# Experts' part without POOL's drain, VectorE's order in the last block, and queries turned ahead of the last value rows

## The reference

```python
x = x + _L0_xattn_ref(_layernorm(x), ctx, ...)        # 16 heads of 64
x = x + _L0_ffn_ref(_layernorm(x), ...)               # 8 experts, top 2, and a shared one
x = x + _L1_xattn_ref(_layernorm(x), ctx, ctx, ...)   # 16 heads of 16
x = x + _L1_ffn_ref(_layernorm(x), weight, bias)      # fp8 rounding with one scale for all of x
```

```python
Qp = query @ Wq + bq
K = _l2norm(key @ Wk + bk); V = value @ Wv + bv; Q = _l2norm(Qp)
attn = softmax(Q K^T / 4) over 16 heads
x = attn V @ Wo + bo + Qp
(x - mean) / sqrt(var + 1e-5) * ln_gamma + ln_beta
```

## Time and profile before

| | before |
|---|---|
| median of 3 runs | 942.38 us (939.27 to 947.75) |
| profiled execution, time | 947.8 us |
| its span | 946.0 us |
| TensorE busy | 867.4 us, 92% |
| VectorE busy | 723.1 us, 76% |
| ScalarE busy | 527.6 us, 56% |
| GpSimd busy | 366.6 us, 39% |

### The profile page before, as it was taken

One profiled execution on the slowest core, in us unless ns is written; L12 is line 12 of the kernel. 1 busy time (PEld: TensorE's weight loads), 2 busy tenths in 40 slices (PEclk: granted clock), 3 DMA queues, 4 the chain that ended last, 5 costly groups with the idle time before them and its releaser, 6 DMA issues. The chain is left out here.

```text
span 946.0 us, 18647 instructions
## 1 busy us (share of the span) xinstructions
PE 867.4 (92%) x5904; PEld 793.7 (84%) x5904; DVE 723.1 (76%) x1821; ACT 527.6 (56%) x1454; POOL 366.6 (39%) x412
## 2 busy tenths in 40 slices
PE   5899999999999999999979999996899999999435
PEld 5889999999999988898978999995688888888324
DVE  6788788878878978878656677784525889877888
ACT  4776567656747645546244444443435566664277
POOL 3234333424333426756521211413544757431230
PEclk9999999999999999999999999997768999999758
DMA  9999970000100013434125434434111111000003
GB/s 287 311 336 326 333 229 0 0 0 0 34 0 1 1 34 96 127 108 140 62 85 146 122 110 148 141 124 122 35 50 35 51 40 46 23 1 2 0 22 156
DMA packets 51771, 91.89 MB, mean 97 GB/s; under 512 B 5381, under 2 KB 26298, under 8 KB 51697
## 3 DMA queue, kind: packets, MB, share of 16 engines
q1 hardware_dynamic: 45105, 72.87, 24.0%
q0 software_dynamic: 6592, 18.07, 6.1%
HBM read 34.56 MB, written 56.36 MB: 96 GB/s over the span
## 5 line engine op out<-in xcount | busy, mean ns | idle before, releaser
L535 POOL TENSOR_TENSOR prob<-prob,row_inv 128x462 f32<-128x462 f32 (+1 forms) x96 | 83.8, 875 | 178.8 <-DVE row_inv L711 178.8
L898 PE MATMUL acc<-u,probT 128*128 128x256 f32 (+1 forms) x960 | 134.2, 289 | 1.0 <-DVE u L723 1.0
L595 ACT ACTIVATE prob<-score,neg_max 128x77 f32<-128x77 f32 x512 | 121.2, 353 | 13.3 <-DVE neg_max L705 12.9
L851 PE MATMUL score<-m,xnT 128*128 128x462 f32 (+1 forms) x576 | 122.7, 350 | 0.0
L898 PEld LDWEIGHTS acc<-u,probT 128*128 128x128 f32 (+1 forms) x960 | 119.5, 189 | 1.9 <-DVE u L723 1.4
L851 PEld LDWEIGHTS score<-m,xnT 128*128 128x128 f32 x576 | 96.3, 188 | 5.8
L2128 PEld LDWEIGHTS acc<-vz,prob 128*128 128x128 f32 (+1 forms) x640 | 82.4, 203 | 13.0 <-issue 11.2
L1231 PE MATMUL py<-w1T,hidT 128*128 x426 | 93.0, 354 | 0.0
L585 ACT ACTIVATE probT<-tr 128x512 fp32r<-128x512 f32 (+1 forms) x96 | 52.0, 545 | 66.2 <-PE tr L837 65.8
L1676 POOL DMA_INDIRECT dispatched<-xn,slots x64 | 69.5, 1085 | 43.8 <-DVEq L1460 26.5
L2128 PE MATMUL acc<-vz,prob 128*128 128x34 f32 (+2 forms) x640 | 84.4, 287 | 0.0
(11 more groups left out here) (381 smaller groups left out, 2100.5 us busy)
## 6 DMA issues: line engine op xcount, KB each, us to landing
dispatched<-zeros SPq DMA_DIRECT2D x1, 33664.0 KB, 109.2
xn<-dispatched SPq DMA_DIRECT2D x71, 128.0 KB, 2.0
dispatched<-hid SPq DMA_DIRECT2D x71, 128.0 KB, 1.8
out<-x_res SPq DMA_DIRECT2D x7, 512.0 KB, 2.6
x_res<-in_x SPq DMA_DIRECT2D x1, 3072.0 KB, 15.2
consts<-in_L_ffn_W SPq DMA_DIRECT2D x8, 384.0 KB, 3.5
consts<-in_L_ffn_Ws SPq DMA_DIRECT2D x3, 384.0 KB, 3.6
x_res<-in_x SPq DMA_DIRECT2D x2, 512.0 KB, 10.2
```

Of the source, the lines that this page charges most:

```text
L535: gp.tensor_tensor(pr, pr, row_inv[t % 2][:, heads(k)].unsqueeze(2).to_broadcast([P, BANK_HEADS[k], KEYS]), ALU.mult).then_inc(prob_ready, 1)
L595: last = act.activation(prob[t % 2][:, h * KEYS:(h + 1) * KEYS], score_of(t, k)[:, n * KEYS:(n + 1) * KEYS], ACT.Exp, bias=neg_max[t % 2][ ...
L851: last = pe.matmul(score_of(t, k)[:, 0:BANK_HEADS[k] * KEYS], xnT[blk][i][:, dc, j * P:(j + 1) * P], m[w][:, dc, cols(k)], start=(n == 0 a ...
L898: last = pe.matmul(acc[t % 2][:, 0:D], probT[t % 2][i][0:rows, c, :], u[k][0:rows, c, :], start=(c == 0 and q == 0), stop=(c == KCH - 1 an ...
```

## The change

Three things are changed. The Block of the experts' part is made without POOL's drain: its barrier then has no `Drain` of POOL, the other engines still drain and report, and POOL still releases them once it has come there itself. In the last block VectorE adds beta for the last two blocks behind the query residual, returns from `dve_block` behind gamma, and does the last units ahead of the shift and update; a maximum of an older block takes the place of a younger one, which moves towards the end. In the opening TensorE turns block 0's queries and does the first scores ahead of value rows 16 to 19, and VectorE splits the queries ahead of the products of these rows.

```diff
-        with nc.Block() as block:
+        with nc.Block(no_gpsimd_drain=True) as block:
...
             dve_query_residual(dve, n)
+            if not nxt:
+                dve_beta(dve, LAST - 1)
+                dve_beta(dve, LAST)
             if nxt:
                 dve_queries(dve, n + 1, 1)
...
             dve_gamma(dve, n - 1, 1)
+            if not nxt:
+                return
             if prv3:
                 dve_last_max(dve, n - 3)
             dve_beta(dve, n - 1)
-            if not nxt:
-                dve_beta(dve, LAST)
             dve_update(dve, n - 1)
...
                 dve_shift(dve, 1)
-                dve_value_rows(dve, range(16, len(SPREAD)))
                 for dc in range(DC):
                     dve_split_q(dve, 0, dc)
+                dve_value_rows(dve, range(16, len(SPREAD)))
                 dve_query_residual(dve, 0)
...
-                dve_last_shift(dve, LAST - 2)
                 for a in range(2):
                     dve_inverse(dve, LAST, 1, a)
                     dve_unit(dve, LAST, 1, a)
+                dve_last_shift(dve, LAST - 2)
+                dve_update(dve, LAST - 1)
                 dve_last_stats(dve, LAST - 1)
-                dve_last_max(dve, LAST - 2)
+                dve_last_max(dve, LAST - 3)
                 dve_residual(dve, LAST, 0)
...
                 dve_last_stats_half(dve, 1)
+                dve_last_max(dve, LAST - 2)
+                dve_last_shift_half(dve, 1)
                 dve_last_max(dve, LAST - 1)
                 dve_last_max_half(dve, 0)
-                dve_last_shift_half(dve, 1)
...
-                pe_value_rows(pe, range(4, len(SPREAD)))
+                pe_value_rows(pe, range(4, 16))
                 for dc in range(DC):
                     pe_transpose_q(pe, 0, dc)
                 pe_scores(pe, 0, 0)
+                pe_value_rows(pe, range(16, len(SPREAD)))
                 pe_first_block(pe)
```

## The result

| | before | changed |
|---|---|---|
| median (14 runs each) | 942.36 us (932.58 to 949.81) | 930.80 us (926.61 to 938.80) |
| profiled execution, time | 947.8 us | 929.04 us |
| its span | 946.0 us | 927.0 us |
| mean granted clock in it | 0.951 | 0.961 |

The account below looks back on a forecast made before the run. TensorE is full in most of the program, so time is won only where it stands still or runs at half speed. Terms -7.0 - 3.9 - 0 to 1.6 - 3.8 against the median 942.4 give 927 us; range 920 to 933.

Parts of the forecast that it names:

- Part 1: Experts' end: without POOL's drain the barrier opens at about 650.5 instead of 657.5, so TensorE starts 7.0 us earlier.
- Part 4: Last block: beta additions hidden in VectorE's idle time, last units wait only for TensorE's last values; -3.8 us.
- Part 2: Opening of the second attention: clock stays up through the shorter pause, so 8.3 us of low-clock work become 4.4; -3.9 us.
- Part 3: Opening: queries turned when ready, rows 16 to 19 behind the first scores; -1.6 to 0 us, nearest prices +0.5 and -2.
- Block 0: Second attention's first block: clock expected to fall again at the turns in most runs, so no gain counted there.
- rival A: Block 0: the clock doesn't fall at all, winning 10 us more, for 921.5 us; chance 0.22.
- B: Experts' end: POOL's 7 us come out again ahead of its next gather, costing 3.7 us, for 931 us; chance 0.12.
- D: Not faster: the clock falls at the turns and stays low until block 1 is over, 953 us; chance 0.02.
- C: Last block: its gain isn't seen, moved additions or ACT's order hold the last units; 3.8 us, 931 us; chance 0.05.

Follow-up runs that it names:

- drain_only: The kernel before with only the experts' Block ended without POOL's drain; 944.30 us, ratio 0.9924 [0.9878, 0.9970].
- no_open_again: The changed kernel with the opening's old order put back, on the second chip; 934.30 us, ratio 0.9848 to the kernel before.
- gathers_late: The kernel before, drain kept, with the experts' part's last six gathers issued in the second attention instead; 957.60 us, ratio 1.0040.
- no_open: The changed kernel with the opening's old order put back, on the first chip; 937.38 us, ratio 0.9881 to the kernel before.
- after_filled: The changed kernel with useless matmuls in TensorE's two waits around the turns of the opening's queries; 920.48 us, ratio 0.9744 to the kernel before.
- before_again: The kernel before itself, unchanged, run and profiled again on the third chip; 943.06 us, ratio 0.9995.
- filled_tail: after_filled with useless matmuls also in TensorE's waits of the last part; 935.86 us, ratio 0.9813 to the kernel before.
- no_open_filled: no_open_again with useless matmuls in the two waits around the first scores; 923.56 us, ratio 0.9771 to the kernel before.
- filled_drain: after_filled with POOL's drain put back at the experts' end; 945.39 us, ratio 0.9897 to the kernel before.
- filled_tail_bar: filled_tail with four 128x128 matmuls on TensorE ahead of the experts' barrier; 934.78 us, ratio 0.9794 to the kernel before.

## Why the prediction was right, and where it was wrong

Parts 1 and 4 came as forecast. What failed is the size of the sum, and in it two steps of the opening: Part 2 took the full clock behind the short pause for certain (-3.9), and Part 3 priced the turned order at -1.6 to 0 against an opening that the other edits had changed. In the profile that goes with the result the two together gave -2.5 us at the second scores, for a forecast of -3.9 to -5.5.

**Part 1, right.** The barrier opened 0.1 us behind SP's drain, and TensorE's pause went from 8.3 to 1.4 us: -6.9 for a forecast of -7.0. drain_only has -7.0 as a whole, with 2.9 to 11.6 allowed by its interval, so that this match is partly luck. POOL gave nothing of it back where anybody waits; its drain at the program's end took 8.50 us instead of 5.46.

What was said to cost nothing did so with less cover than thought. VectorE's first additions started 1.9 us behind the first turn, about as forecast (1.7 us behind the barrier), but took longer. Timeline of VectorE, changed kernel:

```profile
650.98 4.70 DVE L2342 SCALAR_TENSOR_TENSOR x_res<-routed,share,x_res 128x256 f32<-128x256 f32 x4 [2.86 <-DMA routed<-dispatched,slots]
...
656.59 0.68 DVE L2357 TENSOR_TENSOR qp<-proj,bq 128x512 f32<-128x512 f32 x1
...
659.65 1.66 DVE L2342 SCALAR_TENSOR_TENSOR x_res<-routed,share,x_res 128x256 f32<-128x256 f32 x4
```

Four additions took 4.70 us here, and the next four, from 659.65 on, 1.66 us. The excess sits in a single one. All eight of these, by line (ns min/median/max):

```profile
L2342 DVE SCALAR_TENSOR_TENSOR x_res<-routed,share,x_res x8: 475/480/3507, 651.0 to 660.8; 128x256 f32<-128x256 f32 x8
```

It lasted from 651.38 to 654.89. With the drain gone it lies beside POOL's two products at 651.88 and 653.21 (1.39 and 1.38 us). In the kernel before, the first additions lay beside a gather of POOL (658.22) and were over ahead of these products, and took 1.67 us: so the gathers' issue is not what holds them up. The other side of it is a gain: qres took 3.52 us beside the next two of these products, and now comes behind them (671.75) and takes 1.22. The bias on the first queries then starts at 656.59, 1.4 us behind their end (655.2), where I had VectorE free by then. The second half's bias follows at 659.05, 2 us behind its product, so part of the distance to the unit queries is probably VectorE's and not TensorE's. The Trainium skill (SBUF — State Buffer, Who interferes with whom) has the rule that a VectorE instruction with two SBUF inputs contends with a GpSimd instruction that reads SBUF, and the trace agrees: 4.70 us beside POOL's products, 1.66 without. The prediction applied it to the additions of beta, where POOL is idle, and to qres, and not to the one place where the change newly puts the two engines side by side.

**Part 2, the step that failed first.** "The clock was still at 1.00 for 2.9 us after work stopped, so it should now stay up." In 8 of the 12 profiled executions in which the drain was gone or hidden it did. In 4 (the first of the changed kernel, drain_only, no_open_again, gathers_late) it fell within 0.3 us of the first turn, for 3.4, 10.2, 3.4 and 3.4 us. In the first three the unit queries were then turned at +14.91, +19.50 and +16.31, against +13.59 and +14.99 where it stayed. So -3.9 was the best case and not a middle: a fall of 3.4 us cost 1.3 us, one of 10.2 us 4.5. The size where it holds is right: 17.31 - 13.60 = 3.7 in the pair that differs in nothing else ahead of the turns. The Trainium skill (TensorE: Matmul & The Clock Gate, Part 1: The HAM clock gate) says that the chip judges past activity and not program positions; the prediction quoted it, said that the 3.9 us "may be lost again in single runs", and took nothing off for it.

**Part 3, mis-sized, with the wrong base.** It was costed at -1.6 to 0 as a change to a slow opening. Once Parts 1 and 2 are made, the opening as it was is a different one: at full clock rows 16 to 19 take 1.99 us (no_open) and end 1.4 us behind the moment at which the turned order can turn. What is left to win is 1.4 us. In the low clock that comes earlier with it, 2.1 us or more are lost between first and second scores (5.1 to 5.3 us against 3.0 in no_open; it was 3.4 before). The term is +0.7 to +1.4 at the second scores, by three profiles of each order. The bound of the prediction, +0.5, was a little short of it. The second scores came 2.5, 4.0 and 3.3 us nearer to the first turn, for a forecast of 3.9 to 5.5.

**Block 0, right in kind.** The clock fell again about the turns in all three profiles of the changed kernel: with the first scores in two, in the wait ahead of the turns in the third, for 13.7 to 17.1 us, and later for 6.8. So rival A's condition never came about. Its price can't be read directly: after_filled still fell once, for 6.8 us, and from its second scores to block 2's queries it has 28.25 us against 36.89 and 34.12 in the two profiles of before, 8.6 and 5.9 less, for A's 10. The base was a poor one: that profile had 34.2 us at the low clock in block 0, the second 27.4. And A's 921.5 is worked from the profiled 947.8 while the forecast, B and D go by the median; from 942.4 it would have been 916.1, below the range that was to hold it.

**Part 4, right within 0.2 us.** From block 2's queries to x_amax the changed kernel needs 178.72 to 178.74 us in three profiles, and the kernel before 182.30 and 182.39: -3.6, made of -3.8 up to the last turn and +0.2 behind it. From the last values to x_amax it is 19.27 instead of 23.08 us in the first pair, -3.8. The maximum of block LAST-2 stands at 878.58 without a wait ahead of it, as forecast.

**The other rivals.** B is out by POOL's rows above, C by the last turn's 0.81 us, and D by every profile of the changed kernel, whose block 1 was never low to its end: in the first the clock was at 1.00 from 696.95 to 864.23.

**The sum.** From the first turn to the end the changed kernel has 277.93, 276.67 and 277.16 us, before_again 285.71: -7.8 to -9.0, with the pause -14.7 to -15.9, which is the forecast sum. That it comes out is in part luck. Up to the second scores it is -2.5 to -4.0 instead of -3.9 to -5.5, and from there to block 2's queries another -1.8 to -1.9 (32.2 to 32.3 against 34.1), for which the sum had nothing: the shorter falls in block 0 paid for what Parts 2 and 3 lacked. The last part, x_amax to the end, is 0.3 to 0.4 us longer.

The medians have -11.6, -13.6 and -13.8, so 2 to 4 us less than the profiles. The profiled executions of the changed kernel are 0.8 to 2.8 us under their medians, and those of the kernel before 1.2 to 5.4 us above. One cause may be that the unprofiled runs have Part 2's fall more often or for longer. Another may lie in the scatter ahead of the first turn, up to 13 us over all profiles. The mean low fell by 15.4 and 16.3 us in the two later series (71.8 and 69.8 us against 87.2 and 86.1), but that doesn't say where. So the cause of this difference stays open. What a better forecast would have done: give Part 2 half its size, Part 3 zero, and put about 0.3 on "within 1%".

**The better version.** after_filled, at 0.9744 [0.9698, 0.9790] of the kernel before, beats both. It was measured on one chip, with six runs; with fills in the last part as well, which shortened nothing there, filled_tail had 0.9813 [0.9767, 0.9859] on another.

## What to carry to other kernels

Cost an edit to a slow stretch against the stretch as the other edits leave it: of two edits that each hide the same work, the second can be worth nothing. Where TensorE waits 1 to 2 us several times in a row, try a few useless matmuls in these waits before anything is reordered: on the second chip six of them won nearly as much as the three edits together (11.8 us and 13.6). Fill the first of the waits too: where it was left, the clock fell there. And when a span is compared with a span, profile both kernels twice, since one course of the clock was worth 2.8 us in one pair of equal kernels and 11.3 in another, and the part ahead of the change differed by up to 13.

## What the runs showed of the hardware

- POOL's drain at the end of a Block took 0.80 and 1.14 us with no indirect DMA since its last drain, 5.46 with 50, 5.95 with 56, 7.46 with 72, 8.44 with 78 and 8.50 with 128. Leaving it out at one Block lengthened the next one by 3.0 us.
- The granted clock fell in or right behind a pause of 1.3 to 1.4 us in 4 of 12 profiled executions, and in or right behind waits of 1.8 to 2.2 and 0.7 to 1.1 us in all three profiles of the changed kernel. With fills that cut these waits to at most 0.44 and 0.20 us it stayed up through them in all four profiles; in no_open_filled, where only the later waits were filled, it fell.
- The last part (x_amax to the end) took 43.8 us with 15.6 us of low clock in it (filled_tail) and 43.8 with 26.7 (filled_drain, same chip). Over all 18 profiles it took 43.4 to 44.9 us, with 15.6 to 34.6 us low and no order between the two: how long TensorE's clock is low hardly matters there.
- Four additions of 128x256 on VectorE took 4.70 us beside two products of POOL, one of the four 3.51 us instead of 0.48, and 1.67 us beside a gather of POOL.
- TensorE's drain at the experts' end took 0.50 us (filled_tail), and 2.31 us behind four added matmuls of 128x128 (filled_tail_bar).
